# Relation passes of a four-layer graph network: a ring of 48 chunks in place of 32, with its rows in a shared buffer

## The chip, the cores and the metric

The kernel runs on one core of one Trainium2 chip. Its time is the device time in microseconds (us) of that core, from launch to end. Each of the runs shown is a whole execution.

## The reference, cut to what matters

There are four graph layers over 3125 nodes with 256 features and 100000 edges, each followed by a residual and a layer norm. Layers 1 and 3 ("relation layers") are the ones the change touches: every edge takes a row of a table that holds each node's features multiplied by each of 8 weight matrices, and the rows are summed over the edges of a destination (or of a node's own row).

```python
def _L1_gnn_ref(h, basis, w_comp, bias, src, dst, etype):
    ...
    t = jnp.einsum('nd,rdo->rno', h, weight)
    msg = t[etype, src]
    agg = jax.ops.segment_sum(msg, dst, num_segments=h.shape[0])
    return jax.nn.relu(agg + bias)
...
def _L3_gnn_ref(x, edge_index, edge_type, weight, bias):
    row, col = (edge_index[0], edge_index[1])
    xt = jnp.einsum('ni,rio->rno', x, weight)
    messages = xt[edge_type, col]
    out = jax.ops.segment_sum(messages, row, num_segments=num_nodes)
    return jax.nn.relu(out + bias)
```

## The kernel before

Edges are sorted once into chunks of 128, so that all edges of a chunk (or of two chunks, a "unit") go to one tile of 128 nodes. Then stages follow one another, each a block of its own with a barrier of all engines behind it: the spreading of records, the sums of layer 0, the gate, the tables of the first relation layer, its relation pass (`rel1`), the attention layer, the tables of the second relation layer, its relation pass (`rel3`), and the last layer norm.

A relation pass is the function `aggregate`. It is called twice: with k = 0 (832 chunks, two chunks to a unit, so two sums to a group of four chunks) and with k = 1 (808 chunks, one chunk to a unit, so four sums to a group). Chunks are worked on in groups of four (`GRP`). A ring of `ring` groups holds them, and four engines run through it:

- ScalarE (ACT, lines 936 and 937) puts the row numbers and the local destinations of a group into the ring. Before group n it waits until TensorE has summed group n - ring (`act.wait_ge(summed, n - ring + 1)`). This wait is the only thing that holds the ring's writers back.
- GpSimd (POOL, line 944) waits for that staging and issues one indirect DMA for each chunk, which gathers 128 rows of 1 KB from the table into `rows`.
- VectorE (DVE) makes a one-hot matrix of each chunk's destinations (line 965, `build`), `ahead` groups ahead of the sums it adds, and adds each unit's sum from PSUM to the accumulator in SBUF (line 982).
- TensorE (PE, line 956) waits for the four landings and the one-hots of a group and multiplies them, two MATMUL and two LDWEIGHTS rows to a chunk in the profile. It waits for VectorE (`added`) before it uses a PSUM slot again; there are 16 slots.

With `RING = 4` the ring before is `2 * RING` = 8 groups = 32 chunks, and `ahead` is 6 groups. The tile `rows` takes 32 x 256 x 4 bytes = 32 KB of each partition. The other gathering passes (lines 761, 838 and 1913) have rings of `RING` = 4 groups = 16 chunks. `g.big` is a buffer of 26 x 512 floats a partition that other stages use for node features; no instruction of a relation pass reads or writes it before the change.

Of the kernel before, what the change touches and what calls it, by code (L numbers as in the profile page):

```python
# [24 lines left out]
P = 128  # L25
# [13 lines left out]
RING = 4  # L39
# [868 lines left out]
def aggregate(nc, g, tag, k, table, words, word, end, acc):  # L908

    width = words  # L910
    ring = 2 * RING
    body, groups, per = ring * GRP, CHUNKS[k] // GRP, GRP // GRAIN[k]
    ahead, slots = ring - 2, 16
    with ExitStack() as ctx:
        m = Mem(nc, ctx, tag)
        rows = m.sb("rows", [P, body, width])
        hot = m.sb("hot", [P, body, P])
        ring_row = m.sb("ring_row", [P, body], I32)
        ring_end = m.sb("ring_end", [P, body])
        sums = m.ps("sums", [P, slots, 8 * 512 // slots])  # L920
        staged = m.sem("staged")
        hot_ready = m.sem("hot_ready")
        summed = m.sem("summed")
        added = m.sem("added")
        landed = [m.sem(f"landed_{r}") for r in range(ring)]
        block = ctx.enter_context(nc.Block())

        def slot(n):
            return slice(n % ring * GRP, (n % ring + 1) * GRP)

        @block.scalar
        def _(act):
            for n in range(groups):
                if n >= ring:
                    act.wait_ge(summed, n - ring + 1)
                nc.scalar.copy(ring_row[:, slot(n)], g.rec[k][:, n * GRP:(n + 1) * GRP, word])  # L936
                nc.scalar.copy(ring_end[:, slot(n)], g.rec[k][:, n * GRP:(n + 1) * GRP, end]).then_inc(staged, 1)  # L937

        @block.gpsimd
        def _(pool):  # L940
            for n in range(groups):
                pool.wait_ge(staged, n + 1)
                for j in range(slot(n).start, slot(n).stop):
                    pool.indirect_dma_start(rows[:, j, 0:words], None, table, bass.IndirectOffsetOnAxis(  # L944
                        ap=ring_row[:, j:j + 1], axis=0)).then_inc(landed[n % ring], 16)

        @block.tensor
        def _(pe):
            for n in range(groups):
                pe.wait_ge(landed[n % ring], n // ring * (16 * GRP) + 16 * GRP)  # L950
                pe.wait_ge(hot_ready, n + 1)
                for q in range(GRP):
                    j, unit, of = n % ring * GRP + q, n * per + q // GRAIN[k], q % GRAIN[k]
                    if of == 0 and unit % 2 == 0 and unit >= slots:
                        pe.wait_ge(added, unit - slots + 2)
                    last = nc.tensor.matmul(sums[:, unit % slots, 0:width], hot[:, j, :], rows[:, j, :],  # L956
                                            start=of == 0, stop=of == GRAIN[k] - 1)
                last.then_inc(summed, 1)

        @block.vector  # L960
        def _(dve):
            def build(n):
                dve.wait_ge(staged, n + 1)
                for j in range(slot(n).start, slot(n).stop):
                    last = nc.vector.tensor_scalar(hot[:, j, :], g.iota[:, 0:P], ring_end[:, j:j + 1], None,
                                                   ALU.is_equal)
                last.then_inc(hot_ready, 1)

            tiles = []
            for n in range(ahead):  # L970
                build(n)
            for n in range(groups):
                if n + ahead < groups:
                    build(n + ahead)
                dve.wait_ge(summed, n + 1)
                for unit in range(n * per, (n + 1) * per):
                    if unit % 16 == 0:
                        tiles[:] = tiles_of(nc, mybir.EngineType.DVE, g, k, unit)
                    if unit:
                        dve.wait_ge(added, unit)  # L980
                    at = acc[:, bass.ds(tiles[unit % 16], 1), 0:width].rearrange("p t d -> p (t d)")
                    nc.vector.tensor_tensor(at, sums[:, unit % slots, 0:width], at, ALU.add).then_inc(added, 1)  # L982
            dve.wait_ge(added, groups * per)
# [71 lines left out]
def tiles_of(nc, engine, g, k, unit):  # L1055

    return nc.values_load_multi_w_load_instructions(
        g.unit_tile[k][0:1, unit:min(unit + 16, CHUNKS[k] // GRAIN[k])], engines=[engine], min_val=0, max_val=T,
        skip_runtime_bounds_check_because="sort_edges counts them up from 0 and cuts them off at T")[1]
# [1447 lines left out]
def build(nc, a, out):  # L2507
# [8 lines left out]
    with ExitStack() as ctx:  # L2516
# [30 lines left out]
        with ExitStack() as first:  # L2547
            mixer = Mixer(Mem(nc, first, "first"))
            gated_update(nc, g, a, mixer, gate_dram)
            relation_tables(nc, g, a, "mix", t_dram[0], a["L1_gnn_bias"], mixer)  # L2550
        aggregate(nc, g, "rel1", 0, t_dram[0].ap(), D, 1, 2, g.acc)
        hyperbolic_prepare(nc, g, a, msg_dram)
        neighbour_max(nc, g, msg_dram, kept_dram, local_dram)
        attend(nc, g, kept_dram, local_dram, msg_dram)
        finish_and_tables(nc, g, a, o_dram, t_dram[1], a["L3_gnn_bias"])
        aggregate(nc, g, "rel3", 1, t_dram[1].ap(), D, 0, 1, g.acc)
        relu_update(nc, g, "relu3", out=out)

# [21 lines left out]
```

## Time and profile before

| what | value |
|---|---|
| median of 3 runs | 8551.53 us (8549.6 to 8559.96) |
| span of the profiled execution | 8619.9 us, 68.4 us over the median |
| first relation pass, first to last indirect DMA | 4015.0 to 5196.7 us, 832 chunks |
| second relation pass, first to last indirect DMA | 7417.7 to 8568.1 us, 808 chunks |
| busy share of the span | PE 56%, DVE 41%, ACT 20%, POOL 61% |

The profiled execution is one execution, and its own time is its span. An "issue" behind an idle time means that the engine waited for nothing that the profile shows; the releaser behind "<-" is who ended a wait.

### The profile page before, as it was taken

How to read it: one execution, taken by the hardware profiler on the slowest of the kernel's cores; microseconds unless marked ns; L12 is line 12 of the kernel's file. 1: busy time of each engine (PE TensorE's matmuls, PEld its weight loads, DVE VectorE, ACT ScalarE, POOL GpSimd, SP SyncE). 2: the span in 40 equal slices, each digit the busy share in tenths (PEclk: the TensorE clock that was granted, in tenths of full speed). 3: DMA queues.
4: the chain of work that ended last, by engine and by line, in shares of the span. 5: the costliest groups of instructions: out<-in, count | busy, mean ns of one | idle time of the engine just before them, and what ended most of it. 6: DMA issues, size and time to landing. Idle time of an engine off the chain costs nothing. (4 is left out here: it accounts for less than half of the span.)

```text
span 8619.9 us, 69117 instructions
## 1 busy us (share of the span) xinstructions
PE 4852.2 (56%) x17004; PEld 2990.1 (35%) x17004; DVE 3573.0 (41%) x9196; ACT 1730.7 (20%) x7055; POOL 5243.4 (61%) x5610
## 2 busy tenths in 40 slices
PE   3202235555557777777455543777777876655554
PEld 1100014444435555543333332222223663333332
DVE  4201014333335555564222224444445776244445
ACT  0000001111123333322000002222223874000000
POOL 5577756666666666632666662666665882366665
PEclk6655557777778888888666666878888998866666
DMA  3001012222235555554333335656666884333333
GB/s 96 2 3 39 15 40 90 90 89 89 91 116 176 177 175 175 177 114 156 92 93 93 92 93 67 186 184 187 187 187 177 267 271 156 117 93 92 91 94 85
DMA packets 422550, 1037.69 MB, mean 120 GB/s; under 512 B 159993, under 2 KB 188189, under 8 KB 415516
## 3 DMA queue, kind: packets, MB, share of 16 engines
q0 software_dynamic: 223616, 552.46, 22.9%
q1 hardware_dynamic: 198556, 480.95, 17.4%
q8 instruction: 145, 2.38, 0.1%
q14 instruction: 233, 1.91, 0.1%
HBM read 716.74 MB, written 316.30 MB: 120 GB/s over the span
## 5 line engine op out<-in xcount | busy, mean ns | idle before, releaser
L944 POOL DMA_INDIRECT rel_rows<-relation_rows,rel_ring_row x1640 | 1558.3, 950 | 1177.7 <-ACT rel_ring_end L937 695.1
L956 PE MATMUL rel_sums<-rel_rows,rel_hot 128*128 128x256 f32 x3280 | 1197.1, 509 | 1178.3 <-issue 448.5
L956 PEld LDWEIGHTS rel_sums<-rel_rows,rel_hot 128*128 128x128 f32 x3280 | 785.7, 252 | 1590.1 <-issue 1076.9
L982 DVE TENSOR_TENSOR g_acc<-rel_sums,g_acc 128x256 f32 x1224 | 517.8, 423 | 1532.9 <-DMA records_by_dst<-g_big 548.5
L1913 POOL DMA_INDIRECT nmax_rows<-messages,nmax_ring_row x832 | 788.6, 948 | 566.3 <-ACT nmax_ring_row L1869 327.6
L761 POOL DMA_INDIRECT rows_by_src<-spread_rows,spread_ring_place x832 | 803.2, 965 | 483.8 <-issue 254.3
L838 POOL DMA_INDIRECT both_rows<-batch_normed,both_ring_row x832 | 791.0, 951 | 460.9 <-ACT both_ring_end L807 231.3
L605 POOL DMA_INDIRECT records_by_dst<-sort_ring_rec,sort_ring_place x784 | 810.4, 1034 | 390.6 <-issue 241.2
L739 PE MATMUL spread_p_r<-g_big,spread_hot_t 128*128 x1664 | 631.5, 545 | 542.0 <-ACT spread_hot_t L674 358.8
L1961 DVE TENSOR_TENSOR g_big<-nmax_short,g_big 128x512 f32 x832 | 575.7, 692 | 659.9 <-PE nmax_short L1934 288.6
L1934 PE MATMUL nmax_short<-nmax_rows,g_ident_b 128*128 128x512 bf16 x2496 | 800.3, 436 | 0.0
L851 PE MATMUL both_out_sums<-both_out_rows,both_out_hot 128*128 128x257 f32 x1616 | 514.3, 464 | 371.0 <-DVE g_big L886 282.9
L739 PEld LDWEIGHTS spread_p_r<-g_big,spread_hot_t 128*128 128x128 f32 x1664 | 435.4, 274 | 660.1 <-issue 579.6
L1931 PE MATMUL nmax_short<-nmax_away,nmax_minus_ident 128*128 128x512 bf16 x832 | 367.3, 441 | 336.3 <-DVE g_big L1961 205.5
L2073 POOL TENSOR_SCALAR att_hot<-g_iota,g_rec 128x128 f32<-128x128 f32 x624 | 455.5, 746 | 137.3 <-PE att_sums L2137 87.8
L936 ACT CAST rel_ring_row<-g_rec 128x4 int32<-128x4 f32 x410 | 79.4, 194 | 2205.1 <-DMA records_by_dst<-g_big 740.4
L886 DVE TENSOR_TENSOR g_big<-both_out_sums,g_big 128x257 f32 x808 | 343.5, 425 | 413.4 <-remote 179.0
L851 PEld LDWEIGHTS both_out_sums<-both_out_rows,both_out_hot 128*128 128x128 f32 x1616 | 318.6, 221 | 541.7 <-issue 403.8
L860 PE MATMUL both_sums<-both_rows,both_hot 128*128 128x257 f32 x1664 | 430.2, 404 | 16.3 <-issue 16.3
L2096 ACT ACTIVATE att_weighted<-g_big,att_weighted 128x64 f32<-128x64 f32 x1664 | 416.9, 333 | 10.9 <-DMA g_big<-kept_rows 10.4
L1934 PEld LDWEIGHTS nmax_short<-nmax_rows,g_ident_b 128*128 128x128 bf16 x2496 | 273.0, 109 | 352.7 <-issue 148.1
L860 PEld LDWEIGHTS both_sums<-both_rows,both_hot 128*128 128x128 f32 x1664 | 345.5, 208 | 78.9 <-issue 19.2
(443 smaller groups left out, 6114.8 us busy)
## 6 DMA issues: line engine op xcount, KB each, us to landing
kept_rows<-nmax_rows SPq DMA_DIRECT2D x208, 536.0 KB
g_big<-kept_rows SPq DMA_DIRECT2D x208, 536.0 KB
both_out_rows<-rows_by_src SPq DMA_DIRECT2D x202, 520.0 KB
att_local_row<-local_of_edge SPq DMA_DIRECT2D x52, 512.0 KB
rel_rows<-relation_rows,rel_ring_row POOLq DMA_INDIRECT x1640
relation_rows<-mix_table SPq DMA_DIRECT2D x25, 1024.0 KB
relation_rows<-fin_table SPq DMA_DIRECT2D x25, 1024.0 KB, 3.9
rows_by_src<-spread_rows,spread_ring_place POOLq DMA_INDIRECT x832
```

The lines of the kernel that those rows point to most:

```text
L605: pool.indirect_dma_start(rec_dram.ap(), bass.IndirectOffsetOnAxis(ap=ring_place[:, j:j + 1], axis=0), ring_rec[:, j, :], None).then_inc(l ...
L739: last = nc.tensor.matmul(p_r[:, r % 3, q, :], hot_t[:, r % 4, q, :], h_tiles[:, bass.ds(tiles[unit % 16], 1), :].rearrange("p t d -> p (t ...
L761: pool.indirect_dma_start(rows_dram.ap(), bass.IndirectOffsetOnAxis(ap=ring_place[:, j:j + 1], axis=0), rows[:, j, :], None).then_inc(land ...
L838: pool.indirect_dma_start(rows[:, j, 0:D], None, h_dram.ap(), bass.IndirectOffsetOnAxis(ap=ring_row[:, j:j + 1], axis=0)).then_inc(landed[ ...
L851: last = nc.tensor.matmul(out_sums[:, unit % 4, 0:width], out_hot[:, j, :], out_rows[:, j, 0:width], start=of == 0, stop=of == GRAIN[1] - 1)
L860: last = nc.tensor.matmul(sums[:, unit % 4, 0:width], hot[:, j, :], rows[:, j, :], start=of == 0, stop=of == GRAIN[0] - 1)
L944: pool.indirect_dma_start(rows[:, j, 0:words], None, table, bass.IndirectOffsetOnAxis(ap=ring_row[:, j:j + 1], axis=0)).then_inc(landed[n ...
L956: last = nc.tensor.matmul(sums[:, unit % slots, 0:width], hot[:, j, :], rows[:, j, :], start=of == 0, stop=of == GRAIN[k] - 1)
L982: nc.vector.tensor_tensor(at, sums[:, unit % slots, 0:width], at, ALU.add).then_inc(added, 1)
L1913: pool.indirect_dma_start(rows[:, j, :], None, msg_dram.ap(), bass.IndirectOffsetOnAxis(ap=ring_row[:, j:j + 1], axis=0)).then_inc(landed[ ...
L1934: last = nc.tensor.matmul(short[:, q, :, :], g.ident_b[:], halves[:, j, :, part].unsqueeze(2).broadcast_to([P, H, P]), start=False, stop=p ...
L1961: nc.vector.tensor_tensor(at, short[:, c % GRP, :, :], at, ALU.max).then_inc(taken, 1)
```

## The change

The ring of a relation pass becomes 12 groups = 48 chunks, `ahead` becomes 10 groups (it is `ring - 2`), and the gathered rows (48 x 256 floats, 48 KB a partition) lie in the first 12288 of the 13312 floats of `g.big` instead of in a tile of their own. `hot`, `ring_row` and `ring_end` grow by half. The semaphores of the landings become 12 in place of 8.

```diff
@@ -908,12 +908,12 @@
 def aggregate(nc, g, tag, k, table, words, word, end, acc):
 
     width = words
-    ring = 2 * RING
+    ring = 3 * RING
     body, groups, per = ring * GRP, CHUNKS[k] // GRP, GRP // GRAIN[k]
     ahead, slots = ring - 2, 16
     with ExitStack() as ctx:
         m = Mem(nc, ctx, tag)
-        rows = m.sb("rows", [P, body, width])
+        rows = g.big[:, 0:body * width].rearrange("p (c w) -> p c w", w=width)
         hot = m.sb("hot", [P, body, P])
```

On VectorE, at the start of the first relation pass, the program before has these rows (L965 makes one-hots, L1057 loads tile numbers into registers, L982 adds a sum):

```order
L960 UNCONDITIONAL_BRANCH
L965 TENSOR_SCALAR rel_hot<-g_iota,rel_ring_end 128x128 x28
L1057 TENSOR_LOAD g_unit_tile
L982 ISA
L982 TENSOR_TENSOR g_acc<-rel_sums,g_acc 128x256
```

At the same place the changed program has:

```order
L960 UNCONDITIONAL_BRANCH
L965 TENSOR_SCALAR rel_hot<-g_iota,rel_ring_end 128x128 x44
L1057 TENSOR_LOAD g_unit_tile
L982 ISA
L982 TENSOR_TENSOR g_acc<-rel_sums,g_acc 128x256
```

Sixteen one-hots that were built between later sums now stand ahead of the first sum; the second pass shows the same move. On GpSimd, in the first pass, the difference is only where the indirect DMAs write (the new lines name the shared buffer):

```order
 L939 UNCONDITIONAL_BRANCH
-L944 DMA rel_rows<-relation_rows,rel_ring_row 128x256 x832
+L944 DMA g_big<-relation_rows,rel_ring_row 128x256 x832
 L914 UNCONDITIONAL_BRANCH
```

Nothing moved there: the 832 transfers are the same in number, order and shape. The rows of ACT and SP are the same as before.

## Rows read from the trace of the kernel before

**Rows 1.** The page's costliest groups: busy, mean ns of one, idle before them
```profile
L944 POOL DMA_INDIRECT rel_rows<-relation_rows,rel_ring_row x1640 | 1558.3, 950 | 1177.7 <-ACT rel_ring_end L937 695.1
L956 PE MATMUL rel_sums<-rel_rows,rel_hot 128*128 128x256 f32 x3280 | 1197.1, 509 | 1178.3 <-issue 448.5
```

**Rows 2.** Busy time by stretch, inside the two passes: PE, PEld, DVE, ACT, POOL
```profile
4100.00:5150.00 1050.00, 537.00 (x1474) 357.34 (x1475) 293.01 (x1096) 48.78 (x364) 701.40 (x740) 0.67 0.33 93
7540.00:8540.00 1000.00, 512.24 (x1400) 328.70 (x1400) 431.21 (x1401) 44.36 (x352) 665.73 (x701) 0.66 0.32 92
```

**Rows 3.** Indirect DMAs by tile: count, ns, first and last start (rel1, rel3)
```profile
L944 POOL DMA_INDIRECT rel_rows<-relation_rows,rel_ring_row x832: 943/949/1061, 4015.0 to 5196.7; - x167
L944 POOL DMA_INDIRECT rel_rows<-relation_rows,rel_ring_row x808: 943/949/1073, 7417.7 to 8568.1; - x162
```

**Rows 4.** Who GpSimd waited for, us in total, times, longest (rel1, rel3)
```profile
POOL rel_rows L944 <- ACT rel_ring_end L937: 143.5, 41, 6.5
...
POOL rel_rows L944 <- ACT rel_ring_end L937: 149.5, 43, 6.6
```

**Rows 5.** Timeline of GpSimd in rel3, around two neighbouring pauses
```profile
8039.46 0.95 POOL L944 DMA_INDIRECT rel_rows<-relation_rows,rel_ring_row  x1 [0.31 <-issue]
8046.28 0.95 POOL L944 DMA_INDIRECT rel_rows<-relation_rows,rel_ring_row  x1 [5.87 <-ACT rel_ring_end L937]
8047.53 0.95 POOL L944 DMA_INDIRECT rel_rows<-relation_rows,rel_ring_row  x1 [0.30 <-issue]
...
8085.23 0.94 POOL L944 DMA_INDIRECT rel_rows<-relation_rows,rel_ring_row  x1 [0.30 <-issue]
8091.99 0.94 POOL L944 DMA_INDIRECT rel_rows<-relation_rows,rel_ring_row  x1 [5.81 <-ACT rel_ring_end L937]
```

**Rows 6.** Timeline of VectorE and ScalarE in rel3, between those pauses
```profile
8057.48 2.11 DVE L982 TENSOR_TENSOR g_acc<-rel_sums,g_acc 128x256 f32 x4
8062.79 0.42 DVE L982 TENSOR_TENSOR g_acc<-rel_sums,g_acc 128x256 f32 x1 [0.97 <-DVE g_acc L982]
8064.19 0.42 DVE L982 TENSOR_TENSOR g_acc<-rel_sums,g_acc 128x256 f32 x1 [0.97 <-DVE g_acc L982]
...
8059.16 0.19 ACT L936 CAST rel_ring_row<-g_rec 128x4 int32<-128x4 f32 x1 [6.25 <-PE rel_sums L956]
8080.19 0.19 ACT L936 CAST rel_ring_row<-g_rec 128x4 int32<-128x4 f32 x1 [20.74 <-issue]
8091.43 0.19 ACT L936 CAST rel_ring_row<-g_rec 128x4 int32<-128x4 f32 x1 [10.95 <-DMA fin_conv_bias<-in_L_gnn_b_conv]
8091.63 0.19 ACT L936 CAST rel_ring_row<-g_rec 128x4 int32<-128x4 f32 x1
```

**Rows 7.** Timeline in rel1, TensorE one by one, then in a burst after GpSimd's stop
```profile
4339.49 0.58 PE L956 MATMUL rel_sums<-rel_rows,rel_hot 128*128 128x256 f32 x1 [2.22 <-issue]
4340.89 0.28 PEld L956 LDWEIGHTS rel_sums<-rel_rows,rel_hot 128*128 128x128 f32 x1 [2.51 <-issue]
4342.29 0.59 PE L956 MATMUL rel_sums<-rel_rows,rel_hot 128*128 128x256 f32 x1 [2.22 <-issue]
4349.49 0.95 POOL L944 DMA_INDIRECT rel_rows<-relation_rows,rel_ring_row  x1 [0.30 <-issue]
4353.48 9.23 PE L956 MATMUL rel_sums<-rel_rows,rel_hot 128*128 128x256 f32 x30 [2.21 <-issue]
4356.86 0.95 POOL L944 DMA_INDIRECT rel_rows<-relation_rows,rel_ring_row  x1 [6.43 <-ACT rel_ring_end L937]
```

**Rows 8.** The pass of the same form with a ring of 16 (layer 0)
```profile
L838 POOL DMA_INDIRECT both_rows<-batch_normed,both_ring_row x832: 943/949/1075, 2517.2 to 3767.6; - x167
```

**Rows 9.** Timeline at the start of rel1: last issue of group 0, first MATMUL, one-hots
```profile
4018.92 0.95 POOL L944 DMA_INDIRECT rel_rows<-relation_rows,rel_ring_row  x1 [0.30 <-issue]
...
4014.69 5.75 DVE L965 TENSOR_SCALAR rel_hot<-g_iota,rel_ring_end 128x128 f32<-128x128 f32 x28 [6.45 <-ACT rel_ring_end L937]
4021.62 3.78 PE L956 MATMUL rel_sums<-rel_rows,rel_hot 128*128 128x256 f32 x8 [14.64 <-DMA rel_rows<-relation_rows,rel_ring_row]
4026.68 0.99 DVE L982 TENSOR_TENSOR g_acc<-rel_sums,g_acc 128x256 f32 x2 [6.25 <-issue]
```

**Rows 10.** Timeline of VectorE at the end of rel3, last two groups' sums
```profile
8579.41 2.13 DVE L982 TENSOR_TENSOR g_acc<-rel_sums,g_acc 128x256 f32 x4 [0.37 <-DVE g_acc L982]
8581.75 2.13 DVE L982 TENSOR_TENSOR g_acc<-rel_sums,g_acc 128x256 f32 x4 [0.21 <-DVE g_acc L982]
```

## The prediction, made before the changed kernel ran

> **What bounds the kernel now.** I read the page's costliest groups first. The largest is the indirect DMA of the two relation passes, on GpSimd: 1640 of them, 950 ns each, with 1177.7 us of idle time around them [rows 1]. The table by stretch says that inside the passes no engine is near full: of 1050 us in the first, GpSimd is busy 701, TensorE 537, VectorE 293; of 1000 us in the second, 666, 512 and 431 [rows 2]. So the bound is either GpSimd's own rate or a wait in the ring. The timeline of GpSimd separates the two. Undisturbed, one DMA follows the other after 1.25 us (8046.28 to 8047.53: 0.95 busy, 0.30 in "issue") [rows 5]. At that rate 1640 chunks would take 2055 us. They take 1181.7 us (832 chunks, 1.422 us each) and 1150.4 us (808, 1.426 each) [rows 3], 2332 us together. The difference, 277 us, is pauses: the waits for ScalarE's staging are 143.5 us in 41 and 149.5 us in 43 [rows 4]. Each of the 84 has about 0.30 us that an issue takes anyway, so 131 and 137 us are lost, 268 together; the other 9 are short gaps.
>
> What the pauses look like is the key to the change. In the second pass GpSimd restarts at 8046.28 and again at 8091.99 [rows 5], 45.71 us apart. 32 issues at 1.253 take 40.1 us, so the pause adds 5.6: one pause for each filling of the ring of 32. The ring does not fill because transfers are slow. The first group's last DMA is issued at 4018.92 and TensorE starts on it at 4021.62 [rows 9], 2.7 us later; the whole way from a group's first issue to its use is 6.6 us, under two groups of the eight. It fills because the consumers drip. From 8060 on, VectorE's sums, which had come four in 2.11 us (8057.48), come one by one, 1.40 us apart, and ScalarE, which should stage a group every 5 us, stages at 8059.16, then at 8080.19, then at 8091.43 with another right behind at 8091.63 [rows 6]. In the first pass it is TensorE's own instructions that stand 1.40 us apart (4339.49, 4340.89, 4342.29), and they run again, 30 in 9.23 us, from 4353.48, which is 4 us after GpSimd's last issue before its pause, at 4349.49 [rows 7]. In both passes the drip ends only when GpSimd has stopped. What makes the drip these rows don't tell; I use only that it lasts until the ring is full, and that the pause then takes some 5.5 us.
>
> **The change part by part.** *Rows in the shared buffer.* The same 1640 transfers of the same shape to other addresses, and no instruction added: 0 us.
>
> *Prologue.* VectorE builds 44 one-hots ahead of the first sum, not 28. 28 take 5.75 us, so 0.205 each and 9.0 us for 44: from 4014.69 to 4023.7. The first sum starts at 4026.68 [rows 9], so 3 us of cover are left, and 0 is the price. If the cover were gone it would be 3.3 us (16 x 0.205) a pass, but the ring has 12 groups then, so even that delays nothing of GpSimd's. ScalarE stages 12 groups in place of 8 at the start, at 0.2 us each, ahead of GpSimd's 5 us a group: 0.
>
> *The ring.* One pause falls on 48 chunks instead of on 32. Two bounds on what a pause costs then. If it stays as it is, a third of the 268 us goes: 89 us. If it grows with the ring, I need its growth, and the nearest row is the layer-0 pass with a ring of 16: 832 chunks in 1250.4 us [rows 8], 1.505 each, so 0.252 over 1.253, times 16 is 4.0 us a filling. With 32 it is (1.426 - 1.253) x 32 = 5.5. By the same step 48 gives 7.0 us, 0.146 a chunk in place of 0.173: 0.027 x 1640 = 44 us saved. That pass has other work beside it (a second stream of rows), so its pauses may be cheaper or dearer than the ring alone makes them. I take the middle of 44 and 89: 67 us, 33 to 34 in each pass.
>
> *The end of a pass.* TensorE and VectorE may be four groups further behind when GpSimd issues its last. Groups follow each other by 2.34 us there (8579.41 to 8581.75) [rows 10], so 9.4 us at most in the second pass; the first has two sums to a group, so some 5. It depends on where in a period the pass ends; I take a third of the 14: 5 us.
>
> Sum: 67 - 5 = 62 us. The profiled execution's own time would go from 8619.9 to 8558. It is 68.4 us over the median of the runs; I let the same 62 us stand for those: 8551.5 - 62 = 8490 us.
>
> That 68.4 us also says how much of the pauses the recording itself could have made. All five gathering passes have such pauses, 268 us of them in these two alone, so most of them must be in the unrecorded runs too. It leaves room for a smaller gain.
>
> **A rule against the change.** With rows of this case alone a group is in use 6.6 us after its first issue [rows 9], so by latency two groups suffice and eight are plenty. In the Trainium skill, "DMA: Bandwidth & Descriptors", section "Anatomy of one DMA", a DMA from GpSimd's queue takes about 2.0 us and its bytes over 436 GB/s; for 128 KB that is an estimate of 2.3 us, and the trace agrees (2.7 us to the first use). If that were all that the ring covers, the time would stay at 8551 us.
>
> **Rivals.**
>
> *The pause per filling shrinks in number, as above* (forecast). For it: the period equals the ring's length in the second pass, and the costs of a chunk fall from the ring of 16 to that of 32. 8490 us, own range 8455 to 8525. Chance 0.50.
>
> *The drip is paced by time, not by the ring.* After a restart the consumers run freely for some 14 us (8046.28 to 8060) and do five groups at 2.8 us; in the drip and the pause, some 37 us, they do three, one in 12. If these two spans are fixed, a period balances at issued = done, which is eight groups whatever the ring, and the equality with 32 is chance. For it: the free span isn't explained by anything in the ring. Against: in the first pass TensorE could have caught up with any ring. The gain is then 0 to 20 us, about 8545 us. Chance 0.16.
>
> *Nothing changes, since the latency is covered already* (the rule above): 8551 us. Against it are 268 us of waits on the ring. Chance 0.06.
>
> *With 48 chunks of slack most drips are bridged.* If a drip ends by itself some time after it began, a longer ring outlasts it and the pause is gone, not rarer. A drip lasts 20 to 31 us and the four added groups give 20 us of issue. Against: in both stretches shown it ended only behind a stop. Half to all of 268 us go: 8283 to 8420, say 8380 us. Chance 0.14.
>
> *Slower: the drip costs more the longer it lasts.* GpSimd's stop must drain what piled up while it issued. The pauses grew by 1.5 us from a ring of 16 to 32; if from 32 to 48 they grow by more than 2.8 us (5.5 x 48/32 = 8.3), each chunk costs more than before. At 10 us a pause it is 0.208 a chunk, 0.035 x 1640 = 57 us more, and with the tails 14 us: up to 8620, typically 8585 us. Chance 0.14.
>
> **How the numbers follow.** About 0.2% of the time, 17 us, is what a measurement can tell here. Faster by more: the forecast, the bridged drips, and little of the others, 0.64. Within it: the latency rule, most of the time-paced case, and a sliver of the forecast's lower edge, 0.22. Slower: 0.14. The range of 8430 to 8562 leaves out most of the bridged case below and the slower case above, about 2 in 10, and its upper end holds the tails of 14 us without a gain. The likeliest case alone has 8455 to 8525.
>
> **What would show it.** In the changed kernel's profile: GpSimd's spacing stays at 1.25 us; its waits for ScalarE's staging fall to about 200 us of the 293 in both passes; in the second pass restarts are 48 issues, some 66 to 67 us, apart, each with a pause of 6 to 7.5 us; the first pause comes later than the 48th chunk. The 832 chunks take about 1148 us and the 808 about 1117. I am wrong if the restarts stay 32 issues apart (paced by time), if a pause is over 8.3 us (slower), or if pauses are missing. The prologue is wrong if the first sum starts later than 12 us after the pass began.

## The result, and the profile after

The changed kernel takes 8571.9 us (median of 18 runs, 8562.3 to 8582.3) against 8555.1 us for the kernel before (18 runs beside them, 8545.0 to 8567.6): a ratio of 1.002, 95% interval 1.0013 to 1.0026. It is slower by 17 us, where 62 us less was forecast. The span of its profiled execution is 8565.9 us, 54 us shorter than that of before. That is no gain of the change: the first relation pass begins at 3974.3 us in place of 4015.0, after stages that the change does not touch, and another 19 us are saved between the two passes, which it does not touch either. One execution of each is not a comparison of totals; the passes have to be compared by themselves. Even that is not quite fair here: of the kernels profiled below with all their work in them, those on two of the chips start the passes at 3968 to 3984 and 7342 to 7363 us, those on a third at 4005 to 4013 and 7397 to 7402 us. So the two profiles may come from different chips, and a kernel with a ring of 32 that starts its passes where the changed one does is put beside it below (place32).

The groups by cost, of the page after, as in [rows 1]:

```profile
L944 POOL DMA_INDIRECT g_big<-relation_rows,rel_ring_row x1640 | 1553.2, 947 | 1171.3 <-ACT rel_ring_end L937 692.7
L956 PE MATMUL rel_sums<-g_big,rel_hot 128*128 128x256 f32 x3280 | 1142.2, 488 | 1234.1 <-issue 724.2
```

The indirect DMAs by tile of the changed kernel, first and second pass, as in [rows 3], and under them who GpSimd waited for in the same passes, as in [rows 4] (the 360.5 contain the one wait of 214.0 before the first pass):

```profile
L944 POOL DMA_INDIRECT g_big<-relation_rows,rel_ring_row x832: 940/946/1032, 3974.3 to 5152.5; - x167
L944 POOL DMA_INDIRECT g_big<-relation_rows,rel_ring_row x808: 940/946/1069, 7351.7 to 8493.6; - x162
...
POOL g_big L944 <- ACT rel_ring_end L937: 360.5, 39, 214.0
...
POOL g_big L944 <- ACT rel_ring_end L937: 143.9, 45, 6.5
```

The chunks take 1178.2 / 831 = 1.418 us and 1141.9 / 807 = 1.415 us, before 1.422 and 1.426. The waits for staging are 146.5 us in 38 and 143.9 us in 45; less 0.30 for each, 135 and 130 us are lost, before 131 and 137. The waits are 290 us together, where the forecast had about 200. The pauses have not become fewer.

The timeline of GpSimd in the second pass of the changed kernel, as in [rows 5]:

```profile
7992.83 0.94 POOL L944 DMA_INDIRECT g_big<-relation_rows,rel_ring_row  x1 [0.30 <-issue]
7999.48 0.94 POOL L944 DMA_INDIRECT g_big<-relation_rows,rel_ring_row  x1 [5.71 <-ACT rel_ring_end L937]
...
8038.35 0.95 POOL L944 DMA_INDIRECT g_big<-relation_rows,rel_ring_row  x1 [0.30 <-issue]
8045.04 0.94 POOL L944 DMA_INDIRECT g_big<-relation_rows,rel_ring_row  x1 [5.75 <-ACT rel_ring_end L937]
```

With a ring of 48, GpSimd still restarts after 45.6 us, which is 32 issues and a pause of the same 5.5 us. The timeline of ScalarE in the changed kernel shows why (the profile names a DMA of another stage behind two of its waits; in the code it waits for nothing here but TensorE's sums):

```profile
7998.92 0.19 ACT L936 CAST rel_ring_row<-g_rec 128x4 int32<-128x4 f32 x1 [10.95 <-DMA fin_conv_bias<-in_L_gnn_b_conv]
8003.95 0.19 ACT L936 CAST rel_ring_row<-g_rec 128x4 int32<-128x4 f32 x1 [4.17 <-PE rel_sums L956]
8006.71 0.19 ACT L936 CAST rel_ring_row<-g_rec 128x4 int32<-128x4 f32 x1 [2.46 <-PE rel_sums L956]
8011.51 0.19 ACT L936 CAST rel_ring_row<-g_rec 128x4 int32<-128x4 f32 x1 [4.51 <-PE rel_sums L956]
8031.16 0.19 ACT L936 CAST rel_ring_row<-g_rec 128x4 int32<-128x4 f32 x1 [19.36 <-issue]
8044.49 0.19 ACT L936 CAST rel_ring_row<-g_rec 128x4 int32<-128x4 f32 x1 [13.04 <-DMA fin_conv_bias<-in_L_gnn_b_conv]
```

From one stop to the next it stages four groups at once (7998.92 and three right behind it, not shown), then four singly: eight. What GpSimd may issue between two stops is what the consumers finished, not what the ring holds. The longer ring is filled once: the first pause falls behind the 68th chunk, before behind the 48th. After that both run at the same rate, the changed kernel with 48 chunks open in place of 32.

That has a price at the end. Call the time from the start of the last gather to the end of the last sum the tail of a pass. VectorE at the end of the second pass of the changed kernel, as in [rows 10], under GpSimd's last gather:

```profile
8493.65 0.95 POOL L944 DMA_INDIRECT g_big<-relation_rows,rel_ring_row  x1 [0.30 <-issue]
...
8499.98 2.13 DVE L982 TENSOR_TENSOR g_acc<-rel_sums,g_acc 128x256 f32 x4 [6.52 <-DMA fin_conv_bias<-in_L_gnn_b_conv]
8502.80 2.12 DVE L982 TENSOR_TENSOR g_acc<-rel_sums,g_acc 128x256 f32 x4
...
8527.65 2.13 DVE L982 TENSOR_TENSOR g_acc<-rel_sums,g_acc 128x256 f32 x4 [0.21 <-DVE g_acc L982]
```

Twelve such rows, 48 sums, follow the last gather. The tail is 8529.8 - 8493.7 = 36.1 us; before it is 8583.9 - 8568.1 = 15.8 us. From first gather to last sum the second pass takes 1178.1 us, before 1166.2. The first pass, with half as many sums, has a tail of 13.7 us, before 16.5.

The prologue is as worked out: VectorE's 44 one-hots take 9.03 us and the first sum comes 12.0 us after the first one-hot, before 11.99.

```profile
3973.98 9.03 DVE L965 TENSOR_SCALAR rel_hot<-g_iota,rel_ring_end 128x128 f32<-128x128 f32 x44 [6.45 <-ACT rel_ring_end L937]
3986.01 0.99 DVE L982 TENSOR_TENSOR g_acc<-rel_sums,g_acc 128x256 f32 x2 [3.00 <-issue]
```

### The profile page after: what moved, and what is told of

The parts are those of the page before. It is cut to its first block and busy times, and to the rows that moved or that the text cites. A ratio compares the mean times of both kernels' runs of the same rounds, so it can differ in the third digit from the quotient of the medians.

```text
span 8565.9 us, 69117 instructions
## 1 busy us (share of the span) xinstructions
PE 4794.7 (56%) x17004; PEld 2965.4 (35%) x17004; DVE 3570.9 (42%) x9196; ACT 1730.2 (20%) x7055; POOL 5244.4 (61%) x5610
## 5 line engine op out<-in xcount | busy, mean ns | idle before, releaser
L944 POOL DMA_INDIRECT g_big<-relation_rows,rel_ring_row x1640 | 1553.2, 947 | 1171.3 <-ACT rel_ring_end L937 692.7
L956 PE MATMUL rel_sums<-g_big,rel_hot 128*128 128x256 f32 x3280 | 1142.2, 488 | 1234.1 <-issue 724.2
L956 PEld LDWEIGHTS rel_sums<-g_big,rel_hot 128*128 128x128 f32 x3280 | 759.9, 242 | 1617.2 <-issue 1350.3
L982 DVE TENSOR_TENSOR g_acc<-rel_sums,g_acc 128x256 f32 x1224 | 517.8, 423 | 1542.2 <-DMA records_by_dst<-g_big 596.1
L860 PEld LDWEIGHTS both_sums<-both_rows,both_hot 128*128 128x128 f32 x1664 | 345.7, 208 | 77.4 <-issue 13.7
```

The lines of the kernel that those rows point to most:

```text
L860: last = nc.tensor.matmul(sums[:, unit % 4, 0:width], hot[:, j, :], rows[:, j, :], start=of == 0, stop=of == GRAIN[0] - 1)
```

## Experiments

### On one chip: place, a shorter ring, slower issue, gathers alone

Here the kernel before took 8551.2 us (27 runs). The first kernel keeps the ring and takes only the place of the rows from the change:

```diff
     ring = 2 * RING
-        rows = m.sb("rows", [P, body, width])
+        rows = g.big[:, 0:body * width].rearrange("p (c w) -> p c w", w=width)
```

> The rows of the relation passes lie in the shared buffer as in the changed kernel, but the ring stays at 32 chunks. Theory T (a fixed rate of the gathers of about 1.42 us a chunk, and a deeper ring only leaves the consumers further behind at the end of a pass): the buffer's place costs nothing, the time is that of before, 8545 to 8565 us. Rival P (the place of the rows costs the time, by conflicts with other accesses): about 8572 us, as slow as the changed kernel.

It took 8549.7 us, ratio 0.9995 (0.9986 to 1.0004). The place is free. Its second pass is also the fair partner for that of the changed kernel, which starts within 6 us of it: 1144.1 us from first to last gather, 1.418 a chunk, and a tail of 18.9 us (changed kernel: 1141.9 and 36.1).

The second has `ring = RING`, 16 chunks, and nothing else.

> Ring of 16 chunks, rows in their own tile, all else as before. Theory T (fixed rate): no slower than before by more than 20 us, and the tail behind the last gather of the second pass is shorter than the 16 us of before; 8535 to 8575 us. Rival F (the step of my prediction: one pause of 4.0 us for each filling of 16 chunks, 0.252 us a chunk in place of 0.173): 130 us slower, about 8685 us.

It took 8555.5 us, ratio 1.0009 (1.0 to 1.0018). Its chunks in the second pass take 1150.5 / 807 = 1.426 us, as before, and its tail is 14.2 us. Its pauses are smaller and closer (restarts at 8008.83 and 8043.10, each after some 4.5 us). 34.3 us apart means 24 issues and one pause; in its first pass restarts are 28 issues apart. So its period is not its ring's length of 16:

```profile
L944 POOL DMA_INDIRECT rel_rows<-relation_rows,rel_ring_row x808: 943/949/1072, 7352.0 to 8502.5; - x162
...
8008.83 0.94 POOL L944 DMA_INDIRECT rel_rows<-relation_rows,rel_ring_row  x1 [4.52 <-ACT rel_ring_end L937]
8043.10 0.95 POOL L944 DMA_INDIRECT rel_rows<-relation_rows,rel_ring_row  x1 [4.49 <-ACT rel_ring_end L937]
```

That alone refutes the step of my sum. By a pause of 4.0 us a filling it should have been 130 us slower. With 16, 32 and 48 chunks the second pass has 1.426, 1.426 and 1.415 us a chunk; on the chip of this run itself 32 chunks give 1.418 (place32).

The third puts a small memset of a private column behind each gather.

> Behind each gather of the relation passes GpSimd does one small memset of its own (one column of a private tile), which spreads the issues to some 1.38 to 1.45 us in place of 1.25. Ring of 32. Theory T (the gathers pass at 1.42 us a chunk whatever the issue rate): pauses shrink or vanish, the passes keep their length, 8545 to 8600 us. Rival F (pauses come on top of the issue rate, one for each filling): each of 1640 chunks is longer by what the memset takes, 0.13 us or more, so at least 8555 + 213 = 8768 us.

It took 8553.9 us, ratio 1.0005 (0.9995 to 1.0014). It did not spread the issues as it should. The timeline of that kernel shows that the memset fits into the 0.30 us that lie between two gathers anyway:

```profile
4300.77 0.95 POOL L945 DMA_INDIRECT rel_rows<-relation_rows,rel_ring_row  x1 [0.19 <-issue]
4301.72 0.11 POOL L947 MEMSET rel_spin<- 128x1 f32 x1
4302.02 0.95 POOL L945 DMA_INDIRECT rel_rows<-relation_rows,rel_ring_row  x1 [0.19 <-issue]
```

Undisturbed, the gathers still follow each other by 1.25 us. Yet the pauses at the ring shrank: inside the second pass GpSimd waits for staging 74.9 us in 55, none over 2.4 us, where before it is 149.5 in 43 with pauses of 5.5. The pass takes 1147.5 / 807 = 1.422 us a chunk all the same. That is what theory T expects, and what the ring's waits no longer lost came back as short gaps before GpSimd's own instructions. The price by which rival F would have shown itself needs slower issues, so the time alone tells nothing about it.

```profile
POOL rel_rows L945 <- ACT rel_ring_end L938: 74.9, 55, 2.4
```

The fourth leaves the matrix products, the one-hots and the sums out of the relation passes; ScalarE waits for the slot's landings:

```diff
-                    act.wait_ge(summed, n - ring + 1)
+                    act.wait_ge(landed[n % ring], n // ring * (16 * GRP))
```

> The relation passes gather only: no one-hots, no matrix products and no sums are made, ScalarE waits for a slot's landings instead of for TensorE. Theory T (limit in the gathers' own path): some 1.42 us a chunk stay, the passes last 1175 and 1145 us, only the tails go: about 8520 us. Rival C (the consumers' instructions are what drips and holds the ring): the gathers run at GpSimd's 1.25 us, 1042 and 1012 us, and the time falls by some 290 us to 8265 us.

It took 8468.8 us, ratio 0.9906 (0.989 to 0.9921): 82 us less, between the two expectations and nearer to T. In its first pass the 832 gathers take 1135.6 us, 1.367 each, with no wait for staging inside the pass. The first 188 come at 1.25 us, the others at 1.400 on average. One stretch of its timeline on GpSimd:

```profile
4560.55 1.09 POOL L944 DMA_INDIRECT rel_rows<-relation_rows,rel_ring_row  x1 [0.30 <-issue]
4561.95 1.09 POOL L944 DMA_INDIRECT rel_rows<-relation_rows,rel_ring_row  x1 [0.30 <-issue]
4563.35 1.09 POOL L944 DMA_INDIRECT rel_rows<-relation_rows,rel_ring_row  x1 [0.30 <-issue]
```

Exactly 1.40 us lie between them, the step at which the consumers dripped in [rows 6] and [rows 7]. So on this chip gathers are held to one in some 1.40 us even when no one consumes; call this the cap. The drips look like the way in which it reaches the others: while GpSimd is ahead of the cap, someone else's instructions are held back, and with no one else there, GpSimd's. That reading fits all the runs here, but no run tests it.

### On a second chip: less depth, a slower GpSimd again, fewer bytes

The kernel before took 8553.5 us (33 runs). The first is the changed kernel in which ScalarE waits for group n - 8 in place of n - 12; `ahead` stays 10.

> The changed kernel (ring of 48 chunks, rows in the shared buffer, 44 one-hots ahead), but ScalarE waits for group n - 8 instead of n - 12, so that never more than 32 chunks are open. Theory D (depth: the consumers are a ring behind when the last gather is issued, and 12 groups' sums then stand alone): time of before, 8545 to 8560 us, and a tail of some 16 to 19 us in the second pass. Rival S (the cost is in what comes with the longer ring: four more semaphores to clear, longer tiles, the longer prologue): 8572 us as the changed kernel.

It took 8566.0 us, ratio 1.0014 (1.0005 to 1.0023), which looked like S. It was the experiment's own fault. VectorE builds one-hots 10 groups ahead of the group that it adds, and with 8 groups open the staging that this needs comes only when TensorE is three groups past that group. With four sums to a group and 16 PSUM slots that ties the two engines together. (On the fourth chip the same kernel with `ahead` at 6 has the old period and no loss, which bears this out.) In the timeline of its second pass GpSimd stops at 8026.35 and again at 8055.05, every 20 chunks:

```profile
8026.35 0.94 POOL L944 DMA_INDIRECT g_big<-relation_rows,rel_ring_row  x1 [3.98 <-ACT rel_ring_end L937]
8055.05 0.94 POOL L944 DMA_INDIRECT g_big<-relation_rows,rel_ring_row  x1 [3.95 <-ACT rel_ring_end L937]
```

The second holds 32 in the last 24 groups only, with `ahead` 10 again.

> The changed kernel, 48 chunks open but for the last 24 groups of each pass, where 32 are the most. Theory D, tail alone: the time is that of before within 8 us, 8545 to 8563 us, and the tail of the second pass falls from 36 to some 16 to 20 us. If depth costs something along the whole pass as well, it stays at 8565 us or more.

It took 8564.2 us, ratio 1.0013 (1.0004 to 1.0022), a tail of 20.8 us. It has the same fault in its last 24 groups and settles nothing.

The third has three memsets behind each gather, to spread the issues beyond the cap.

> Ring of 32 as before, with three small memsets on GpSimd behind each gather of the relation passes, which spreads the issues to about 1.5 us (one memset fitted into the 0.30 us between two gathers and changed nothing). Theory T (some path passes a gather per 1.40 us at most, pauses come only where GpSimd issues faster): no pauses are left, and the time grows by what 1.5 is over 1.43 a chunk, 0.07 x 1640 = 115 us, to about 8670 us. Rival F (pauses of 5.5 us a ring come on top of any issue rate): 0.25 x 1640 = 410 us more, 8960 us.

It took 8562.4 us, ratio 1.0011 (1.0001 to 1.002). The 8670 us of its expectation did not come, since three memsets fit in almost as well as one: undisturbed, the gathers are 1.27 us apart, not 1.5. What changed is who is held back. GpSimd has no wait for ScalarE inside the passes at all; its own instructions have the gaps now, of 0.6 to 0.8 us:

```profile
8001.53 0.94 POOL L945 DMA_INDIRECT rel_rows<-relation_rows,rel_ring_row  x1 [0.82 <-issue]
8002.72 0.14 POOL L949 MEMSET rel_spin<- 128x1 bf16 x2 [0.24 <-issue]
8003.44 0.10 POOL L949 MEMSET rel_spin<- 128x1 bf16 x1 [0.59 <-issue]
8004.35 0.94 POOL L945 DMA_INDIRECT rel_rows<-relation_rows,rel_ring_row  x1 [0.81 <-issue]
```

All the pauses at the ring are gone and the time is 9 us longer. The pauses at the ring were not a cost of their own.

The fourth gathers 512 bytes a row in place of 1024 (other rows of the table; the second half of each ring row is zero, so the sums are not the reference's).

> As before with a ring of 32, but each gathered row has 512 bytes in place of 1024 (half of a row of the table; the other half of each row in the ring is zero, so the sums are not the reference's). As many gathers, rows and instructions of the consumers. Theory B (the path is limited in bytes): the gathers run at 1.25 us without pauses and the time falls by some 250 us to 8300 us. Rival R (limited by the number of DMAs, rows or updates): 8540 to 8565 us, with the pauses as before.

It took 8559.4 us, ratio 1.0008 (0.9999 to 1.0018); its second pass has 1144.1 / 807 = 1.418 us a chunk and waits for staging of 142.6 us in 31. The cap is not in bytes, and not in the DMA packets that the trace records either: a gather has 32 there in place of 48 (16 of them hold 4 bytes each).

```profile
L947 POOL DMA_INDIRECT rel_rows<-relation_rows,rel_ring_row x808: 942/947/1044, 7345.0 to 8489.1; - x162
...
POOL rel_rows L947 <- ACT rel_ring_end L938: 142.6, 31, 5.9
```

### On a third chip, which has no cap

The mended kernels set `ahead` to 6 groups. held32b is the changed kernel with at most 32 chunks open, ahead6 has 48 open, capend6 holds 32 in the last 24 groups. The edit of held32b (ahead6 is its first hunk alone):

```diff
-    ahead, slots = ring - 2, 16
+    ahead, slots = 2 * RING - 2, 16
...
-                if n >= ring:
-                    act.wait_ge(summed, n - ring + 1)
+                if n >= 2 * RING:
+                    act.wait_ge(summed, n - 2 * RING + 1)
```

> The changed kernel (ring of 48 chunks in memory, rows in the shared buffer, 12 landing semaphores), with at most 32 chunks open and the one-hots 6 groups ahead as before. held32 kept the one-hots 10 groups ahead, which made VectorE wait for sums three groups on; that is mended here. Theory D (the 17 us come from depth, as a longer tail): 8545 to 8560 us, tail of the second pass 15 to 19 us. Rival S (longer tiles, more semaphores): 8565 to 8575 us.

> The changed kernel with 48 chunks open, only the one-hots again 6 groups ahead in place of 10. Theory D: depth is unchanged, so it is as slow as the changed kernel, 8565 to 8575 us, with a tail of some 36 to 39 us in the second pass (four more groups of one-hots fall into it). Rival H (the one-hots that stand further ahead cost the time): 8550 to 8558 us.

> 48 chunks open up to the last 24 groups of each pass, 32 in those, one-hots 6 groups ahead throughout. Theory D: all of the cost of depth is the tail, so the time of before, 8547 to 8560 us, tail 15 to 19 us in the second pass. If it is 8565 us or more, depth costs along the way.

On this chip the kernel before itself took 7621.9 us (27 runs), 11% less than on the first two. The three took 7622.4, 7623.0 and 7621.5 us, ratios 1.0001, 1.0 and 1.0001, each within 0.0009 either way. The last kernel is the one that only gathers, with 64 rows a DMA:

> The kernel that only gathers (8469 us), each indirect DMA with 64 rows in place of 128: as many DMAs, half the rows and packets. Theory R (the cap of 1.40 us a gather is in rows or packets): GpSimd's own rate is left, 1.25 us or less a gather, at least 1640 x 0.11 = 180 us faster than 8469, under 8290 us. Rival N (the cap is in the number of DMAs or their 16 semaphore updates): 1.40 us a gather stay, 8455 to 8480 us.

It took 7523.7 us, ratio 0.9871 (0.9856 to 0.9886). A gather of 64 rows takes GpSimd 0.90 us in place of 0.95. Since there was no cap here, it cannot tell what the cap counts.

Four more kernels ran on the same chip, the changed kernel among them: before 7621.7 us (33 runs), the four 7622.3, 7623.1, 7620.7 and 7621.2 us, ratios 1.0, 1.0001, 1.0 and 0.9999. capend6 ran on no other chip, so whether the whole cost of depth is in the tail was not tried with it.

> The changed kernel as it is. If the gathers are capped (before near 8553 us): 8565 to 8577 us, tail of the second pass some 36 us. If they are not (before near 7622 us), the ring never fills with either size, and the ring of 48 changes nothing: within 8 us of before, tail of 14 to 15 us.

> Ring of 48 in memory, at most 32 chunks open, one-hots 6 groups ahead. Capped, theory D (depth makes the tail): 8545 to 8560 us, tail of the second pass 15 to 20 us. Capped, rival S (semaphores and longer tiles): 8565 to 8575 us. Uncapped: 7622 us within 8.

> 48 chunks open, one-hots 6 groups ahead. Capped, theory D: as slow as the changed kernel, 8565 to 8575 us, tail of the second pass 36 to 40 us. Capped, rival H (one-hots ahead cost the time): 8550 to 8558 us. Uncapped: 7622 us within 8.

> 48 chunks open but in the last 24 groups of each pass, 32 there, one-hots 6 groups ahead. Capped, theory D with all of the cost in the tail: 8547 to 8560 us, tail of the second pass 15 to 20 us; at 8565 us or more, depth costs along the way. Uncapped: 7622 us within 8.

The changed kernel's second pass there, by tile, and what GpSimd waited for in it:

```profile
L944 POOL DMA_INDIRECT g_big<-relation_rows,rel_ring_row x808: 942/946/1073, 6556.4 to 7567.9; - x162
...
POOL g_big L944 <- ACT rel_ring_end L937: 4.3, 14, 0.3
```

1011.5 / 807 = 1.253 us a chunk, GpSimd's own rate from the first gather to the last, with 4.3 us of waits, none over 0.3. The tail is 14.2 us. The same program gives 1.415 and 36.1 us on the chip of the first profile. Without the cap the ring never fills here, and its length means nothing.

### On a fourth chip, under the cap: the two that tell the 17 us apart

The kernel before took 8602.4 us (20 runs) here.

> As held32b_again. Where before takes near 8553 us: theory D 8545 to 8560 us with a tail of 15 to 20 us in the second pass, rival S 8565 to 8575 us. Where before takes near 7622 us: 7622 us within 8.

> As ahead6_again. Where before takes near 8553 us: theory D 8565 to 8575 us with a tail of 36 to 40 us in the second pass, rival H 8550 to 8558 us. Where before takes near 7622 us: 7622 us within 8.

With 32 chunks open: 8604.3 us, ratio 1.0004 (0.9995 to 1.0013), no slower than before. With 48 open: 8620.9 us, ratio 1.0025 (1.0016 to 1.0035), 18.5 us slower, as the changed kernel was. The two differ in the one wait. The second pass by tile, last gather and last sum, first of the kernel with 32 open, then of that with 48:

```profile
L982 DVE TENSOR_TENSOR g_acc<-rel_sums,g_acc x808: 408/424/426, 7413.9 to 8569.6; 128x256 f32 x162
L944 POOL DMA_INDIRECT g_big<-relation_rows,rel_ring_row x808: 940/946/1076, 7402.0 to 8550.2; - x162
```

```profile
L982 DVE TENSOR_TENSOR g_acc<-rel_sums,g_acc x808: 405/424/426, 7408.7 to 8579.7; 128x256 f32 x162
L944 POOL DMA_INDIRECT g_big<-relation_rows,rel_ring_row x808: 940/946/1072, 7397.0 to 8542.5; - x162
```

The last sums start 19.4 and 37.2 us behind the last gathers. The gathers themselves take 1148.2 and 1145.5 us. So depth gives 3 us on the way and takes 18 at the end. The first passes differ by 1 us (1197.9 and 1198.8 from first gather to the start of the last sum). Together that is 16 us, and the two times are 16.5 apart. The one-hots that stand further ahead, the semaphores and the longer tiles cost nothing that shows.

No version that does the whole work beat the kernel before by more than the noise on any chip.

## Why the prediction was wrong

**The bound.** The rate of 1.42 us a chunk against GpSimd's 1.25 was read rightly, and so was the size of the pauses, 268 us. The 68.4 us by which the profiled execution of before was longer raised the question whether they are in the timed runs. They are: the profiled execution of the changed kernel took 8567.7 us, inside the 8562.3 to 8582.3 of its timed runs, with 265 us lost in such pauses.

**The step that failed.** "One pause falls on 48 chunks instead of on 32": my sum took the ring's length for the cause of the period, because 45.7 us fitted 32 issues and one pause. The period is what the consumers finish between two stops: in the second pass eight groups with 8 or with 12 groups of ring, six groups with 4. The trace of before had a sign of this that I did not read. In its first pass, with the same ring of 32, no two neighbouring restarts (after waits of over 2.5 us) are 32 issues apart: 16 of the 31 distances are 36, as from 4465.37 to 4516.03, the others 4, 8, 16 or 40:

```profile
4465.37 0.95 POOL L944 DMA_INDIRECT rel_rows<-relation_rows,rel_ring_row  x1 [6.43 <-ACT rel_ring_end L937]
4516.03 0.95 POOL L944 DMA_INDIRECT rel_rows<-relation_rows,rel_ring_row  x1 [5.82 <-ACT rel_ring_end L937]
```

So in the second pass the period equalled the ring by chance. The growth of the pause that I drew from the layer-0 pass with its ring of 16 priced the same false cause: what that pass costs above the others (1.505 us a chunk) is not its ring. ring16 is the direct test: 0.079 us a chunk expected more, 0.000 to 0.008 measured (against before and place32). Of the saving of 67 us next to nothing came: from first to last gather the two passes take 2320 us together with 48 chunks open and 2319 with 32 (place32), or 2323 and 2328 on the fourth chip.

**The rival that was nearer.** "The drip is paced by time, not by the ring" gave restarts 32 issues apart, which is what the trace after shows and what I had named as the sign of being wrong. I gave it 0.16. Its gain of 0 to 20 us did not come either, since it left out the tail. The evidence for it was in my own view: the first pass has two sums a group and the second four, VectorE is busy 293 and 431 us [rows 2], and yet a chunk costs 1.422 and 1.426 us [rows 3]. A limit that doesn't move with the consumers' work points at the gathers themselves. The rival's account by free and dripping spans was not tested; gatheronly, slowissue and pace3 speak for a cap on the gathers instead.

**The term that was mis-sized.** The tails were priced at 5 us, a third of 14. The second pass's is 20 us longer; the first's is 3 us shorter by the two profiles and 3 us longer by the pair of the fourth chip. I took four more groups as the most, but 12 groups were left against the five full ones of before. Four of the seven are what a deeper ring can add. The rest is where the pass happens to end: before had stopped for its ring 16 chunks before the end, the changed kernel 32 chunks before its end, a whole period. With a ring of 32 the tail is 15.8 us 16 chunks behind the last stop, and 18.9 and 19.8 us 20 chunks behind it (place32, held32b on the fourth chip); both kernels with 48 open ended 32 chunks behind it, with 36.1 and 37.6 us. So a part of the 17 us is bad luck with the number of chunks. How large a part, no run shows: none with 48 open ended elsewhere in a period.

**The rest.** Rows in the shared buffer: 0 us, shown by place32. Prologue: 9.0 us worked out, 9.03 measured, hidden. The rule of the Trainium skill that I set against the change ("DMA: Bandwidth & Descriptors", section "Anatomy of one DMA": about 2.0 us and the bytes over 436 GB/s for a DMA) made it a change without effect. The traces agree with the rule: the last packet of a gather ends 2.4 us after the gather starts on GpSimd, before and after. By rows, latency needed two groups of ring; ring16 shows that four do as well as eight. "Nothing changes" was 17 us off under the cap, nearer than the forecast, and exact on the chip without it; its chance of 0.06 was too low. The slower rival (pauses that grow with the ring) ended on the right side by the wrong mechanism: the pauses stayed at 5.5 us. The bridged drips did not come either: the second pass has 24 waits of over 2.5 us, before 25.

**What stays open.** What the cap of 1.40 us counts. Not the bytes or packets (halfrows), not the consumers' work (gatheronly, and the two passes against each other), not GpSimd's own issue (the same instructions run at 1.25 us on the third chip), not the ring. Nor are the transfers late: in both passes of before the last packet of a gather ends 2.4 us after its start in the median, and within 2.7 us for 95% of them (the last 30 of a pass left out), as on the chip without the cap. Rows and semaphore updates of a gather are left, and rows64, which should have told them apart, met no cap. One more rival was not tested, the recording itself. A gather adds 16 to its semaphore, in 16 updates. On the chip without the cap the profile of the second pass has a record of each, 12928 for 808 gathers. Under the cap it has 1623 before and 1655 after, one in eight, and 1591 to 3285 in the other runs of whole passes. Records are missing where the cap is, and nowhere else. Whether an execution that records nothing has the cap, no run shows; every timed execution here comes with a granted clock, so something of each was recorded. Nor was it tried why one chip has none. That the drip moves from the consumers to GpSimd when GpSimd has more instructions was seen (pace3), not explained.

## What to carry to other kernels

A ring that is found full, and a period that equals its length, do not say that the ring is too short: count what the consumer finishes between two stops, look whether the period is the same in another pass with the same ring, and ask whether the rate is the same where the consumer has less to do. If the rate is the same, a deeper ring is likely to move no rate: here it was filled once, and left up to its whole depth to be worked off alone when the producer ended. A shorter ring is the cheapest test of a longer one.

## What the runs showed of the hardware

- Indirect DMAs of 128 rows from GpSimd: 0.95 us busy and 0.30 us between two. One memset of a column in that gap leaves the spacing at 1.25 us, three make it 1.27.
- Three of the four chips of the experiments held these gathers to a mean of 1.41 to 1.43 us with consumers; on the one of them where it was tried without consumers, it was 1.40 us after the first 188. The other chip ran all of them at 1.25 us, and took 7622 us for a program that took 8551 to 8602 us on the three.
- The last packet of a gather ended 2.4 us after its start (median), under the cap and without it. Under the cap the trace holds about one in eight of the records of the gathers' semaphore updates (1623 of 12928 in the second pass of before), without it all of them.
- Under the cap other engines' instructions come in steps of 1.40 us ([rows 6], [rows 7]), and when GpSimd alone works, its gathers do, with 1.09 us busy in place of 0.95.
- Half the bytes a row changed neither the rate (1.418 us a chunk) nor the busy time (0.95 us), under the cap; half the rows, tried without it, took 0.90 us in place of 0.95.
